# Attention probabilities through DRAM in one piece per unit, new weights multiplied high parts first, and two steps moved on VectorE

## What is computed

```python
xn = layernorm(x)                                  # x: (2, 512, 512)
q, k, v = xn @ Wq.T, xn @ Wk.T, xn @ Wv.T          # 32 query heads, 8 key heads, head size 128
q, k = rmsnorm(q) * q_norm_w, rmsnorm(k) * k_norm_w
scores = q @ k.T / sqrt(128) + slope[head] * (pos_k - pos_q), masked above the diagonal
s = softmax(scores) @ v, then @ Wo.T
low = xn @ A.T (8 experts, rank 16); route = 8 * softmax(xn @ Wr.T + br)
g = silu(2 * sum over experts of route * (low @ B.T))
return x + s * g
```

## Time and profile before

| | |
|---|---|
| median of three runs | 746.49 us (745.05 to 747.19) |
| time of the profiled execution | 747.09 us |
| span of its profile | 745.3 us |
| TensorE busy | 720.7 us, 97% |
| VectorE busy | 600.7 us, 81% |
| ScalarE busy | 560.5 us, 75% |
| GpSimd busy | 332.9 us, 45% |
| SyncE's DMA queue | 184224 packets, 130.39 MB |

### The profile page before, as it was taken

How to read it: one execution, slowest core, us unless ns; L and a number is a source line. 1 busy time by engine, 2 the same in 40 slices (tenths; PEclk the granted TensorE clock), 3 DMA queues, 4 the chain that set the end, 5 groups by cost and what they waited for, 6 DMA issues and landing times.

```text
span 745.3 us, 14609 instructions
## 1 busy us (share of the span) xinstructions
PE 720.7 (97%) x3741; PEld 605.6 (81%) x3741; DVE 600.7 (81%) x1490; ACT 560.5 (75%) x1440; POOL 332.9 (45%) x320
## 2 busy tenths in 40 slices
PE   7999999999999999999999999999999999999997
PEld 6787878878788888888788887888788788888866
DVE  7867898688887889697987889777986879868976
ACT  4566878687877878777876877778787778769972
POOL 4223444354334633644344543437326443445656
PEclk9999999999999999999999999999999999999999
DMA  8015968678695877868686786958677686867761
GB/s 302 2 29 148 276 164 238 194 224 239 162 277 146 227 214 220 233 168 268 165 237 191 221 243 158 286 140 234 202 222 223 177 270 161 242 179 209 202 184 70
DMA packets 214773, 148.02 MB, mean 199 GB/s; under 512 B 48992, under 2 KB 205536, under 8 KB 214624
## 3 DMA queue, kind: packets, MB, share of 16 engines
q1 hardware_dynamic: 184224, 130.39, 60.1%
q10 hardware_dynamic: 30528, 17.38, 9.5%
HBM read 85.84 MB, written 61.87 MB: 198 GB/s over the span
## 4 chain that ended last, share of the span: by engine, by line
PE 52%; DVE 14%; issue 11%; DMA 9%; ACT 6%; POOL 6%; SPq 2%; DVEq 0%; ACTq 0%; POOLq 0%
PE qkv_ps L1364 5%; PE qkv_ps L1365 5%; PE qkv_ps L1366 5%; DMA x_sb<-turning 4%; PE out_ps L1364 4%; PE out_ps L1366 4%; PE out_ps L1365 4%; PE score_ps L1364 4%; PE score_ps L1366 3%; PE score_ps L1365 3%; DVE squared L1039 3%; POOL pt_lo L589 2%; PE mix_ps L1364 2%; PE mix_ps L1366 2%; PE mix_ps L1365 2%
## 5 line engine op out<-in xcount | busy, mean ns | idle before, releaser
L589 POOL TENSOR_TENSOR pt_lo<-x_sb,pt_hi 128x512 fp32r<-128x512 f32 x129 | 164.2, 1295 | 255.4 <-ACT pt_hi L795 255.4
L720 ACT ACTIVATE probs<-probs,neg_max 128x128 f32<-128x128 f32 (+3 forms) x256 | 142.2, 559 | 39.6 <-DVE neg_max L1018 38.3
L1018 DVE CUSTOM_DVE_ANT_0 probs<-score_ps,cst,slope 128x128 f32<-128x128 f32 (+3 forms) x256 | 131.1, 544 | 27.9 <-PE score_ps L1366 27.4
L728 ACT ACTIVATE probs<-probs,recip 128x128 f32<-128x128 f32 (+3 forms) x252 | 126.1, 549 | 8.0 <-DVE recip L1025 8.0
L1364 PE MATMUL qkv_ps<-w_hi,xt_hi 128*128 128x256 f32 (+1 forms) x392 | 126.0, 321 | 3.1 <-DVE xt_lo L961 1.7
L1365 PE MATMUL qkv_ps<-w_lo,xt_hi 128*128 128x256 f32 (+1 forms) x392 | 125.7, 321 | 0.0
L1366 PE MATMUL qkv_ps<-w_hi,xt_lo 128*128 128x256 f32 (+1 forms) x392 | 125.2, 319 | 0.0
L795 ACT ACTIVATE pt_hi<-x_sb 128x512 fp32r<-128x512 f32 x153 | 86.6, 624 | 48.3 <-issue 31.1
L1364 PE MATMUL out_ps<-wo_hi,o_hi 128*128 128x512 f32 x252 | 102.5, 407 | 2.2 <-DVE o_lo L1063 1.9
L1039 DVE STREAM_TRANSPOSE squared<-probs 128x256 f32<-128x256 f32 (+3 forms) x124 | 101.8, 822 | 0.3 <-ACT probs L728 0.3
L579 POOL TENSOR_TENSOR inv_rms<-sums,minus_half 128x5 f32<-128x5 f32 x64 | 76.4, 1193 | 57.5 <-DVE sums L1077 57.5
(11 more groups left out here) (191 smaller groups left out, 1589.9 us busy)
## 6 DMA issues: line engine op xcount, KB each, us to landing
qk_moved<-turning_qk SPq DMA_DIRECT2D x60, 320.0 KB, 3.4
turning_qk<-qk_squared ACTq DMA_DIRECT2D x212, 80.0 KB, 2.0
turning<-squared SPq DMA_DIRECT2D x120, 128.0 KB, 2.4
x_sb<-turning SPq DMA_DIRECT2D x30, 512.0 KB, 4.9
w_raw<-wqkv SPq DMA_DIRECT2D x32, 384.0 KB, 5.3
turning<-squared SPq DMA_DIRECT2D x120, 96.0 KB, 2.0
x_sb<-turning SPq DMA_DIRECT2D x30, 384.0 KB, 4.3
turning<-squared SPq DMA_DIRECT2D x128, 64.0 KB, 1.8
```

The lines of the kernel that those rows point to most:

```text
L589: nc.gpsimd.tensor_tensor(by_quad(pt_lo, j), moved_block(t, j), by_quad(pt_hi, j).bitcast(F32), ALU.subtract).then_inc(pt_lo_by_pool, 1)
L720: nc.scalar.activation(probs[:, h, 0:n], probs[:, h, 0:n], ACT.Exp, bias=neg_max[:, h:h + 1], scale=-1.0, accum_out=total[:, h:h + 1]).the ...
L728: nc.scalar.activation(to[:, h, 0:n], probs[:, h, 0:n], ACT.Copy, scale=recip[:, h:h + 1]).then_inc(probs_ready, 1)
L1018: nc.vector.tensor_tensor_reduce(probs[:, h, 0:n], score_bank(t, h), cst[:, C_DIST + SEQ - n:C_DIST + SEQ], slope[:, h:h + 1], HUGE, ALU.a ...
```

## The change

- `squared` is filled densely, and SyncE writes both pairs of heads of a unit together: it waits for both halves of `square_probs`, issues four DMAs (each twice as large as before, rows twice as long), then reads q and k, waits for the four writes, and reads everything back with one DMA. The condition `keys_of(t) <= QB` holds for every unit, so the old path isn't used. The counters follow (`WRITTEN`, `MOVED`).
- `project` of unit 8 multiplies all high parts of the new weights first (`project_new`): q of the four chunks, then k and v of the four, and then the matmuls with the low parts chunk by chunk. The number and the sizes of the matmuls stay.
- `add_out` of unit t-3 comes after the first half of `square_probs` and after `turned_qk_lo`; in slot 5 after both halves.
- In the last group `multiply_gate` starts one slot earlier, and the last two blocks are multiplied after `mixed_lo` of unit 6 instead of before it; the first two tanh come before the normalisation.

```diff
-WRITTEN = counter([16 * QUADS] * BLOCKS)
-MOVED = counter([32] * BLOCKS)
+WRITTEN = counter([16 * QUADS] * BLOCKS), counter([0] * BLOCKS)
+MOVED = counter([16] * BLOCKS)
...
+                if keys_of(t) <= QB:
+                    if soon and u is not None:
+                        sp.wait_ge(qk_lo_ready, K_AND_Q_LO(g, u, 0))
+                        read_qk(g, u)
+                    write_all_probs(g, t)
+                    if u is not None and not soon:
+                        read_qk(g, u)
+                    sp.wait_ge(probs_written[0], WRITTEN[0](g, t, 16 * QUADS))
+                    sp.dma_start(moved_whole(t), turning[t % 2, :, :, 0:2 * n].rearrange("q p n -> p q n")).then_inc(probs_moved, 16)
+                    return
...
+            def write_all_probs(g, t):
+                n = keys_of(t) * P
+                sp.wait_ge(probs_squared, TWO(g, t, 2))
+                for q in range(QUADS):
+                    sp.dma_start(turning[t % 2, q, :, 0:n].rearrange("(k r) n -> r k n", k=QUADS),
+                                 squared_whole[q * QUAD:(q + 1) * QUAD, :, 0:n]).then_inc(probs_written[0], 16)
...
-                add_out(g, t - 3)
                 square_probs(g, t, 0)
                 turned_qk_lo(g, t + 1)
                 square_probs(g, t, 2)
+                add_out(g, t - 3)
...
-                if left == 1 and t == 4:
-                    multiply_gate(range(0, 2))
+                if left == 1 and t in (3, 4):
+                    multiply_gate(range(2 * (t - 3), 2 * (t - 3) + 2))
...
-                if here(t - 3, left):
-                    add_out(g, t - 3)
                 if here(t, left):
                     square_probs(g, t, 0)
                 if here(t + 1, left):
                     turned_qk_lo(g, t + 1)
+                if here(t - 3, left):
+                    add_out(g, t - 3)
...
-                multiply_gate(range(4, 6))
                 add_out(g, before - 1)
+                mixed_lo(g, before, 1)
                 multiply_gate(range(6, BLOCKS))
-                mixed_lo(g, before, 1)
...
+            def project_new(g, t):
...
+                parts = ((q_ps(t), slice(0, QW)), (qkv_ps[:, 1, 0:QKV - QW], slice(QW, QKV)))
+                for k, (to, cols) in enumerate(parts):
...
+                    for c in range(KC):
+                        if k == 0:
+                            pe.wait_ge(w_hi_done, (g + t // BLOCKS) * KC + (c + 1))
+                        pe.matmul(to, xt_hi[:, c, rows], w_hi[:, c, cols], start=c == 0, stop=False)
+                        pe.matmul(to, xt_lo[:, c, rows], w_hi[:, c, cols], start=False, stop=False)
+                for c in range(KC):
...
+                    for (to, cols), done in zip(parts, (q_ready, kv_ready)):
+                        last = pe.matmul(to, xt_hi[:, c, rows], w_lo[:, c, cols], start=False, stop=c == KC - 1)
```

More of the change, by code:

```diff
@@ L411, in last_turns, with moved_whole @@
             return sum(keys_of(u) for u in range(BY_PE, t))
+        def moved_whole(t):
+            return moved[t % 2].rearrange("p q s n -> p q (s n)")[:, :, 0:keys_of(t) * P]
         def moved_block(t, j):
+            if keys_of(t) <= QB:
+                return moved_whole(t).rearrange("p q (s n) -> p q s n", s=2)[:, :, :, j * P // 2:(j + 1) * P // 2]
             return moved[t % 2][:, :, :, j * P // 2:(j + 1) * P // 2]
@@ L468, in move @@
                                      qk_squared[q * QUAD:(q + 1) * QUAD, :, :]).then_inc(qk_written, 16)
+                if keys_of(t) <= QB:
+                    if soon and u is not None:
[7 more added lines that the diff above has]
+                    return
                 write_probs(g, t, 0)
-                if soon:
+                if soon and u is not None:
                     sp.wait_ge(qk_lo_ready, K_AND_Q_LO(g, u, 0))
@@ L476, in move @@
                 for pair in range(2):
-                    sp.wait_ge(probs_written[pair], WRITTEN(g, t, 16 * QUADS))
+                    sp.wait_ge(probs_written[pair], WRITTEN[pair](g, t, 16 * QUADS))
                     sp.dma_start(to[:, :, pair, 0:n],
                                  turning[t % 2, :, :, pair * n:(pair + 1) * n].rearrange("q p n -> p q n")).then_inc(probs_moved, 16)
+            def write_all_probs(g, t):
[4 more added lines that the diff above has]
+                                 squared_whole[q * QUAD:(q + 1) * QUAD, :, 0:n]).then_inc(probs_written[0], 16)
             def write_probs(g, t, pair):
@@ L789, in moved_hi @@
             def moved_hi(g, t):
-                act.wait_ge(probs_moved, MOVED(g, t, 32))
+                act.wait_ge(probs_moved, MOVED(g, t + 1, 0))
                 if t > 0:
@@ L815, in slot @@
                     exponentials(g, t, range(0, HPG))
+                if left == 1 and t == 3:
+                    gate_tangents(range(0, 2))
                 if w_due:
@@ L821, in slot @@
                     normalize_probs(g, t, range(0, 2))
-                if left == 1 and t == 3:
-                    gate_tangents(range(0, 2))
                 if left == 1 and t == 4:
@@ L846, in end @@
                 for pair in range(2):
-                    act.wait_ge(probs_written[pair], WRITTEN(g, before, 0))
+                    act.wait_ge(probs_written[pair], WRITTEN[pair](g, before, 0))
                 normalize_probs(g, before, range(0, 2), late_probs)
@@ L1031, in square_probs @@
                 if t > 0:
-                    dve.wait_ge(probs_written[h // 2], WRITTEN(g, t, 0))
+                    dve.wait_ge(probs_written[h // 2], WRITTEN[h // 2](g, t, 0))
                 if t >= 2 and h == 2:
@@ L1037, in square_probs @@
                         dve.wait_ge(moved_lo_by_dve, DVE_BLOCKS(g, t - 1, 0))
-                blocks = squared[:, :, h // 2, :].rearrange("p k (j h n) -> p h j k n", j=QB, h=HPG // 2)
-                nc.vector.transpose(blocks[:, :, 0:keys_of(t), :, :],
+                if keys_of(t) <= QB:
+                    part = squared_whole[:, :, h // 2 * n // 2:(h // 2 + 1) * n // 2]
+                else:
+                    part = squared[:, :, h // 2, 0:n // 2]
+                nc.vector.transpose(part.rearrange("p k (j h n) -> p h j k n", j=keys_of(t), h=HPG // 2),
                                     probs[:, h:h + 2, 0:n].rearrange("p h (j k n) -> p h j k n", k=QUADS, n=QUAD)).then_inc(probs_squared, 1)
@@ L1242, in end @@
                 add_out(g, before - 3)
-                multiply_gate(range(2, 4))
+                multiply_gate(range(4, 6))
                 mixed_lo(g, before - 2, 1)
@@ L1404, in project_kv @@
                     last.then_inc(kv_ready, 1)
+            def project_new(g, t):
+                m = t % BLOCKS
+                rows = slice(m * P, (m + 1) * P)
+                parts = ((q_ps(t), slice(0, QW)), (qkv_ps[:, 1, 0:QKV - QW], slice(QW, QKV)))
+                for k, (to, cols) in enumerate(parts):
+                    if k == 1:
+                        pe.wait_ge(k_norm_ready, ONE(g, t - 1, 1))
+                        pe.wait_ge(v_lo_ready, ONE(g, t - 1, 1))
+                    for c in range(KC):
[4 more added lines that the diff above has]
+                for c in range(KC):
+                    if c < W_DVE:
+                        pe.wait_ge(w_lo_by_dve, (g + t // BLOCKS - 1) * W_DVE + (c + 1))
+                    else:
+                        pe.wait_ge(w_lo_by_pool, (g + t // BLOCKS - 1) * (KC - W_DVE) + (c - W_DVE + 1))
+                    for (to, cols), done in zip(parts, (q_ready, kv_ready)):
+                        last = pe.matmul(to, xt_hi[:, c, rows], w_lo[:, c, cols], start=False, stop=c == KC - 1)
+                        if c == KC - 1:
+                            last.then_inc(done, 1)
             def project(g, t, chunks=range(KC)):
@@ L1413, in project @@
                 elif two_banks(t):
[L1414 to L1420, removed]
+                    project_new(g, t)
                 else:
```

1 line of the change is left out of this document (added).

## The result

| | before | after |
|---|---|---|
| median, same chip | 746.84 us (745.05 to 747.66, four runs) | 780.89 us (780.84 to 781.35, four runs) |
| ratio, 95% interval | | 1.0443 [1.0407, 1.0479] |
| span of the profiled execution | 745.3 us | 779.0 us |

The change makes the kernel 34 us slower. That is the forecast's sign, but three times its size (+12), and outside the range of 743 to 768.

A forecast was written before the change was run, and what follows sets the result against it. TensorE was taken as the bound, time lying only in its gaps. Seven times 1.03 + 0.96 lost (13.9), less 1.9 gained, made +12.0 us: 758.5 us against the median of 746.49, range 743 to 768.

The forecast's parts named there:

- What bounds the kernel: TensorE works 97% of the span; its gaps at slot 5's end (1.08 us) follow unit 3's probabilities; unit 7 has 0.64 spare.
- X: Later landing of a four-block unit's probabilities, counted from the end of `square_probs`' second half: 1.6 us, between 0.1 and 4.
- I take the row they are nearest to, 267 GB/s: Rate assumed for the four doubled writes of probabilities, making them land 1.8 us later.
- I take 0.2 us saved: One 1 MB read of probabilities instead of two: 0.2 us saved, ends 0.5 saved and 1.3 lost.
- Unit 3: End of slot 5: k_lo comes X later less 0.57 for the moved `add_out`, 1.03 us lost, seven times.
- Unit 7: Before `mix`: X less the 0.64 us of slack, 0.96 us lost, seven times.
- q and k of unit 1: After unit 1: earlier turned q and k remove three waits of 0.4 us each, 1.2 us gained.
- The projection, narrow units, the end: `project_new` gives nothing by itself; units under four blocks cost nothing; the o_lo wait at the end gives 0.7 us.
- The faster one: Rival: the writes flow like y's store, X is 0.1, 5.2 us gained, 741.3 us; chance 0.20.
- in between: Rival: X from 0.6 to 0.9, losses and gains cancel, 744 to 748.7 us; chance 0.09.
- The third: Rival: the single read is quick, only q and k are late, unit 7 costs nothing, 751.6 us; chance 0.10.
- The fourth, no overlap at all: Rival: X is 2.6 and more, 26 us lost, 772 us; chance 0.06.

The follow-up runs named there:

- only4: The changed kernel with the new transport only for units of four key blocks, the others in two pairs as before: 781.33 us, 1.0449 of before.
- thr3: The changed kernel, but units of four key blocks go in two pairs as before, one to three blocks in one piece: 742.30 us, 0.9925 of before.
- order0213: The changed kernel with its four writes in the order of quarters 0, 2, 1, 3: 774.57 us, 1.0344 of before.
- qk_first: The changed kernel with the read of q and k issued ahead of the four writes of probabilities: 818.38 us, 1.0941 of before.
- qk_between: `others_alone` with the read of q and k issued between the two reads of probabilities: 749.70 us, 1.0033 of before.
- no_hi_first: `others_alone` with the projection of unit 8 back in its old order, chunk by chunk: 739.90 us, 0.9925 of before.
- transport_alone: The kernel before with the new writes and single read for every unit and no other edit: 791.32 us, 1.0566 of before.
- others_alone: The changed kernel with the old transport, two writes and two reads for every unit, all other edits kept: 741.16 us, 0.9901 of before.
- others_0213: `others_alone` with all writes of quarters, probabilities and q, k, in the order 0, 2, 1, 3: 740.46 us, 0.9923 of before.
- dma_alone: A kernel without any computation that times writes and reads of one tile on an idle core: four quarters of 256 KB took 5.97 us.
- one_read: The changed kernel with the probabilities written per pair of heads as before, only the read in one piece: 750.21 us, 1.0028 of before.

## Why the prediction was right in sign and wrong in size, point by point

**What bounds the kernel: right.** The loss is in TensorE's gaps, at the places named. `only4` and `thr3` show that the transport of units 3 and 7 alone carries it.

**X, the term that failed.** The prediction took X = 1.8 for the writes less 0.2 for the read, 1.6; the runs show 3.0. By its own formula, 14 x 3.0 - 10.4 = +32 us, where +34 was measured. Both terms were mis-sized, about equally. The writes cost 2.5 us more, not 1.8 (medians 6.25 against 3.7). The read costs 0.4 us more, not 0.2 less: the one read takes 5.8 us at unit 3 and 5.5 at unit 7, the second read of before 5.4 and 5.0. So the steps that failed are "I take the row they are nearest to, 267 GB/s" and "I take 0.2 us saved".

For the writes, the 267 was read where eight 128 KB writes followed one another, and on the idle core it holds for such writes (267) and not for four of 256 KB (214; in the changed kernel 203). The prediction treated its three readings (222, 257, 267) as one rate with noise and took the top one. Its bound for 222 was reckoned wrongly too: the fixed part of 1.73 us belongs to 267. At 222 it is 3.69 - 2.36 = 1.33, and the writes take 1.33 + 4.72 = 6.05 us, not 6.45. Measured were 5.97 idle and 6.25 in the kernel.

For the read, the 4.9 us was taken for the second read of a pair, but the row is the median of all 30, first and second. The second ones alone have 5.4, the first ones 4.8. A read of 1 MB in one piece takes 5.6 in the median of after and 5.1 to 5.6 on the idle core.

**What 1 us of X costs: right.** The formula says 14 us. In `order0213` the probabilities come 0.5 to 0.6 us sooner and the time falls by 6.8 us. But q and k come sooner there too, as they come later in the changed kernel, so the price holds for both together.

**Unit 3: right in kind.** X - 0.57 would be 2.4 us with X = 3.0; 2.2 were lost in slots 4 to 6. But 1.49 us of the 3.19 now stand at the start of slot 5, before unit 5's scores: q and k, whose read is behind the bigger writes. Their q_hi begins 7.8 us after the squares instead of 5.9. The prediction said that this overlaps with the loss at unit 3 and isn't added, and the total agrees; which of the two would remain if the other were mended wasn't shown, as neither `qk_first` nor `qk_between` moved q and k alone. One sign was not met: ScalarE's idle time before `moved_hi` was to be some 2 and 3 us and is 1.6 and 2.05 in the median (0.4 and 1.55 before); ScalarE, which now waits longer for q and k ahead of it, comes to it later itself.

**Unit 7: right,** place, wait (pt_lo before `mix`) and price. The last block of its `mix` begins 422.13 - 404.43 = 17.70 us after its squares, before 315.82 - 300.58 = 15.24: 2.46 us later, where X - 0.64 is 2.4.

**q and k of unit 1: missed.** The read of these q and k is behind unit 7's writes, and TensorE waits 0.50 us for k_lo before unit 1's scores in slot 1 of the next group. The prediction had a gain here, three times 0.4 us.

**The projection, narrow units, the end: right.** Taking `project_new` back costs nothing (`no_hi_first`), units of one to three blocks cost nothing measurable (`thr3`), and the wait for w_lo went while that for k_lo stayed. That X could stop TensorE at the last w_hi, "inside the shadow of k_lo", came as said: 0.82 us before chunk 3, and k_lo 0.39 after it. At the end 0.7 us of gain was given; the last stretch is 2.2 us shorter than before and 0.8 shorter than in `transport_alone` (30.1), which lacks this edit.

**`add_out`: right, if anything small.** 7 x 0.57 + 1.2 = 5.2 us was given; taking it back costs 1.0006 - 0.9901 = 0.0105, 7.8 us, with 3 us of uncertainty. All edits but the transport were put at 1.9 + 7 x 0.57 = 5.9 us; `others_alone` gained 0.0099, 7.4 us.

**The rivals.** The faster one needed the rate of y's store, 385 GB/s; the 214 GB/s on the idle core rule it out, and X = 3.0 rules out "in between". The third said that the single read is quick and that unit 7 costs nothing; neither came. The fourth, no overlap at all (772 us from X = 2.6), was the nearest, and had a chance of 0.06. The range ended at 768 although the prediction's own slower bounds, 2.8 for the writes and 1.3 for the read, reach X = 4.1; even with its bound for 222 GB/s set right (2.4) and only the middle of the read's bounds (0.4), X is 2.8.

The advice that follows is to keep the writes of each half and both reads: `others_alone` and `no_hi_first`, at 0.990 and 0.9925, and `others_0213` at 0.9923 are the fastest kernels of this study and can't be told apart.

## What to carry to other kernels

A transfer that is cut so that its first half leaves while the second is still being made was worth more than half as many packets of twice the length: here joining the halves brought the data 3 us late, 14 times, and each us of that cost the kernel some 13 (1.0443 against 0.9901 for 3.1 us). A median over all DMAs of one kind hides that the second of two in flight lands later than the first. Price a DMA by the partitions that it reaches, with the slowest rate that the trace shows for that shape, and let the range reach to it. In a queue that works in order, a moved transfer brings its wait along for everything behind it.

## What the runs showed of the hardware

- Four DMAs of 256 KB, each from 32 partitions: 5.97 us; each from 128 partitions: 4.11 us; one DMA of 1 MB from 128 partitions: 4.42 us (all on an idle core, `dma_alone`).
- Added to four DMAs of 128 KB from 32 partitions, 0.52 MB cost 1.96 us as four more DMAs (267 GB/s) and 2.45 us as twice the size of each (214 GB/s).
- The order 0, 2, 1, 3 of the 32-partition quarters takes 5.32 us instead of 5.97 with the same bytes and packets, and in the kernel 6.8 us less (774.57 against 781.33).
- Packets of 2 KB in place of 1 KB brought no speed for these quarters: eight DMAs of 128 KB (`pairs`) took 5.48 us, four of 256 KB 5.97.
- TensorE's granted clock fell to 1.2 GHz from 73.0 to 76.4 us after a wait of 2.07 us (after), from 73.6 to 77.0 after one of 3.00 (`one_read`), and not after one of 0.96 at the same place (`others_alone`).
